# Staging weights in other buffers and spreading their splitting into the first block: a fused Mamba and mixture-of-experts layer on one Trainium2 core

## The reference

```python
xn = _layernorm(x)
# branch 1: Mamba (E = 512 channels, N = 16 states, 4 convolution taps)
hidden, gate = split(einsum('blh,he->bel', xn, W_in))
hidden = silu(causal_conv(hidden) + conv_bias)
dt, Bm, Cm = split(einsum('ble,ed->bld', hidden^T, W_x))
dts = softplus(dt @ W_dt + b_dt)
state = exp(dts * A) * state + dts * Bm * hidden      # over time, for 16 states
y = (sum over states of state * Cm + hidden * D) * silu(gate)
out1 = y @ W_out
# branch 2: top-8 of 32 experts, evaluated densely with zero weights for the rest
probs = softmax(xn @ router_w.T);  rw, sel = top_k(probs, 8);  rw = rw / sum(rw)
for e in experts: acc += silu(xn @ w_gate[e]) * (xn @ w_up[e]) @ w_down[e] * w_e
return x + out1 + acc
```

## Time and profile before

| | us |
|---|---|
| median of 3 runs | 1395.14 (1394.36 to 1397.05) |
| profiled execution, its own time | 1396.65 |
| its span | 1394.8 |
| outside the span | 1.85 |
| PE busy | 1319.1 (95%) |
| POOL busy | 1243.4 (89%) |
| DVE busy | 1233.4 (88%) |
| ACT busy | 1215.1 (87%) |

### The profile page before, as it was taken

How to read it: one execution, slowest core, us unless ns; L and a number is a source line. 1 busy time by engine, 2 the same in 40 slices (tenths; PEclk the granted TensorE clock), 3 DMA queues, 4 the chain that set the end, 5 groups by cost and what they waited for, 6 DMA issues and landing times.

```text
span 1394.8 us, 26557 instructions
## 1 busy us (share of the span) xinstructions
PE 1319.1 (95%) x9314; PEld 1237.2 (89%) x9314; DVE 1233.4 (88%) x1580; ACT 1215.1 (87%) x2054; POOL 1243.4 (89%) x641
## 2 busy tenths in 40 slices
PE   2499999999999999999999999999999999999998
PEld 2389998999989999999989999898999989999987
DVE  4498989999899999989899898999989899898886
ACT  3799988989998898888989998888989989998884
POOL 3689998999989998999998989898998989999996
PEclk9899999999999999999999999999999999999999
DMA  6634444434444444344434444433343443434342
GB/s 158 171 96 129 119 124 130 118 116 122 124 115 125 124 115 131 112 136 119 127 113 126 128 113 125 130 113 120 114 135 110 129 120 118 134 108 131 118 133 68
DMA packets 184531, 170.74 MB, mean 122 GB/s; under 512 B 42672, under 2 KB 167632, under 8 KB 184400
## 3 DMA queue, kind: packets, MB, share of 16 engines
q1 hardware_dynamic: 150608, 121.86, 30.0%
q10 hardware_dynamic: 33792, 47.20, 12.5%
HBM read 163.72 MB, written 5.24 MB: 121 GB/s over the span
## 4 chain that ended last, share of the span: by engine, by line
PE 30%; ACT 25%; DVE 20%; issue 13%; POOL 10%; ACTq 1%; DMA 1%; SPq 0%; DVEq 0%; POOLq 0%
PE pair_ps L851 12%; ACT decay L553 8%; PE out_ps L969 7%; DVE state L752 7%; ACT L553 6%; POOL state L467 4%; DVE u L769 3%; DVE moe L776 3%; DVE acc L759 3%; PE front_ps L851 3%; PE turn_ps L931 3%; PE front_ps L894 2%; ACT L561 2%; ACT moe L561 2%; POOL moe L482 2%
## 5 line engine op out<-in xcount | busy, mean ns | idle before, releaser
L752 DVE TENSOR_TENSOR_SCAN state<-decay,state 128x512 f32<-128x512 f32 x512 | 616.0, 1214 | 95.0 <-ACT decay L553 88.5
L467 POOL TENSOR_TENSOR state<-du,b_rep 128x1024 f32<-128x1024 f32 x256 | 608.0, 2384 | 72.0 <-DVE u L769 71.8
L553 ACT ACTIVATE decay<-dt,neg_a 128x255 f32<-128x255 f32 x1024 | 437.0, 467 | 61.6 <-DVE state L752 47.1
L969 PE MATMUL out_ps<-w_down,moe 128*128 128x256 f32 x1536 | 353.2, 379 | 2.0 <-POOL moe L482 2.0
L969 PEld LDWEIGHTS out_ps<-w_down,moe 128*128 128x128 f32 x1536 | 284.4, 190 | 38.4 <-issue 3.6
L482 POOL TENSOR_TENSOR moe<-moe,rw_rep 128x512 f32<-128x512 f32 x192 | 260.3, 1367 | 22.6 <-DVE moe L776 22.2
L476 POOL TENSOR_TENSOR state<-state,c_rep 128x1024 f32<-128x1024 f32 x96 | 251.7, 2622 | 11.0 <-DVE state L752 10.9
L851 PE MATMUL pair_ps<-xnT_hi,w_up_hi 128*128 128x256 f32 x768 | 232.8, 303 | 15.9 <-ACT moe L561 13.5
L851 PE MATMUL pair_ps<-xnT_hi,w_gate_hi 128*128 128x256 f32 x768 | 229.5, 299 | 7.1 <-DVE moe L776 7.1
L553 ACT ACT_TABLE_LOAD x176 | 225.8, 1283 | 3.2
L851 PE MATMUL pair_ps<-xnT_hi,w_up_lo 128*128 128x256 f32 x768 | 217.6, 283 | 0.0
(11 more groups left out here) (97 smaller groups left out, 2095.2 us busy)
## 6 DMA issues: line engine op xcount, KB each, us to landing
w_down<-in_L_ffn_w_down_dram SPq DMA_DIRECT2D x384, 128.0 KB, 2.5
b_rep<-b_dram ACTq DMA_DIRECT2D x128, 256.0 KB, 3.5
rw_rep<-rw_dram SPq DMA_DIRECT2D x256, 96.0 KB, 2.7
rw_rep<-rw_dram SPq DMA_DIRECT2D x256, 64.0 KB, 2.7
c_rep<-b_dram ACTq DMA_DIRECT2D x96, 128.0 KB, 3.0
rw_rep<-rw_dram SPq DMA_DIRECT2D x256, 32.0 KB, 2.5
x_in<-L_attn_input_states_dram SPq DMA_DIRECT2D x16, 256.0 KB, 3.3
res<-L_attn_input_states_dram SPq DMA_DIRECT2D x16, 256.0 KB, 3.6
```

Of the source, the lines that this page charges most:

```text
L467: pool.tensor_tensor(state[:, n % STATES, :, :], du2[:, q, :, :], b_rep[:, n // BCH % 2, n % BCH, :][:, None, :].broadcast_to([P, ET, T]), ...
L553: last = act.activation(decay[:, h, j, 1:T], dt[:, q, e, 1:T], ACT.Exp, scale=neg_a[:, e, n:n + 1])
L752: dve.tensor_tensor_scan(x, decay[:, h, :, :].rearrange("p e t -> p (e t)"), x, 0.0, ALU.mult, ALU.add).then_inc(scanned, 1)
L969: last = pe.matmul(out_ps[:, c, :], moe[:, p % RING, j, c * P:(c + 1) * P], w_down[:, p % RING, j, :], start=(p == 0 and j == 0 and c == 0 ...
```

## The change

Three things are changed together.

1. `staging` is six buffers instead of four: the halves of `u2`, `dt` and `du2` that the odd blocks use, `gate2`, and two halves of `w_down`. Piece k goes to buffer k mod 6. None of these is used by block 0 before its middle.
2. The waits follow the buffers. POOL's first `state_input` no longer waits for the splits. In its place SP waits for all splits ahead of the first loads of `w_down`, ACT ahead of `hid0` of block 1 and ahead of the first gate. On SP the load of x for block 1 moves to just before piece 9's, and that of `w_out` to just behind piece 17's. Splits may stand in block 0's own slots.
3. All slot tables hold new numbers, for the splits and for the work of every block.

```diff
-    UNIT_AT = [0, 2, 8, 24, 30, 33, 42, 44, 47, 55, 55, 56, 56, 61, 70, 84, 87, 102, 102, 107, 107, 112, 119, 119]
+    UNIT_AT = [-5, 1, 6, 18, 18, 28, 37, 41, 41, 53, 54, 57, 61, 61, 64, 85, 86, 87, 112, 113, 114, 115, 119, 121]
...
-    SPLIT_VECTOR_AT = [-109, -101, -93, -90, -69, -46, -44, -37, -36]
-    SPLIT_SCALAR_AT = [-126, -113, -108, -106, -106, -96, -95, -68, -65, -60, -53, -46, -39, -39, -36, -26, -23, -20]
-    SPLIT_POOL_AT = [-107, -101, -101, -92, -69, -69, -32, -29, -18]
+    SPLIT_VECTOR_AT = [-124, -96, -91, -56, -51, -35, -35, -5, 14]
+    SPLIT_SCALAR_AT = [-124, -119, -103, -99, -81, -78, -77, -77, -58, -39, -37, -37, -30, -22, -3, -1, 4, 11]
+    SPLIT_POOL_AT = [-102, -96, -86, -84, -64, -57, -37, -6, 7]
...
-        staging = [state[:, m, :, :].rearrange("p e t -> p (e t)") for m in range(STATES)]
+        staging = [x[:, 1, :, :].rearrange("p e t -> p (e t)") for x in (u2, dt, du2)]
+        staging.append(gate2[:, :, :].rearrange("p e t -> p (e t)"))
+        STAGED_DOWN = UT * P // WGROUPS
+        staging += [w_down[:, :, :, :].rearrange("p r j h -> p (r j h)")[:, m * STAGED_DOWN:(m + 1) * STAGED_DOWN] for m in range(2)]
...
+                if k == 9:
+                    sp.wait_ge(front_filled, 1)
+                    load_x(1)
+            sp.dma_start(w_out[:, :, :], w_out_d.rearrange("(k p) h -> p k h", p=P)).then_inc(w_late_loaded, 16)
             sp.wait_ge(rw_stored, 16)
             for p in range(WEIGHTS - 1):
                 load_rw(0, p)
+            wait_split(sp, len(splits))
             for p in range(RING):
                 load_down(p)
-            sp.wait_ge(front_filled, 1)
-            load_x(1)
-            sp.dma_start(w_out[:, :, :], w_out_d.rearrange("(k p) h -> p k h", p=P)).then_inc(w_late_loaded, 16)
...
                 if n == 0:
                     pool.wait_ge(du_ready, i + 1)
-                    if first_pair(i):
-                        wait_split(pool, len(splits))
...
+                    if name == "hid0" and i == 1:
+                        wait_split(act, len(splits))
...
+                if half == 0 and first_pair(i):
+                    wait_split(act, len(splits))
...
+            def split_scalar(k):
+                act.wait_ge(staged[k % len(staging)], (k // len(staging) + 1) * 16)
+                act.activation(splits[k][0], staged_part(k), ACT.Copy).then_inc(split_hi, 1)
```

More of the change, by code:

```diff
@@ L79, in build @@
-    GATE_AT = [44, 56]
-    SILU_AT = [-2, 13, 24, 36, 44, 48, 63, 75, 92, 95, 112, 115]
-    SCALAR_FRONT = {'xnT': -115, 'hid0': -107, 'hid1': -99, 'weightsT': -64, 'low': -53, 'lowT': -50, 'dt0': -44, 'dt1': -32}
-    CONV_SILU_AT, ROUTER_EXP_AT, SOFTPLUS_AT, FIRST_AT, SKIP_AT = [-66, -86, -23, 4, 19]
-    GATE_SILU_AT = [46, 62]
-    MUL_AT = [14, 29, 45, 49, 56, 63, 77, 89, 106, 110, 124, 129]
-    ADD_AT = [[23, 27], [36, 37], [52, 59], [72, 74], [81, 93], [101, 109], [113, 116], [123, 126], [130, 132]]
@@ L102, in build @@
-    SPLIT_POOL_AT = [-107, -101, -101, -92, -69, -69, -32, -29, -18]
+    UNIT_AT = [-5, 1, 6, 18, 18, 28, 37, 41, 41, 53, 54, 57, 61, 61, 64, 85, 86, 87, 112, 113, 114, 115, 119, 121]
+    OUT_AT = [38, 38, 46, 61, 74, 98, 99, 101, 117, 124, 141, 145]
+    TURN_AT = [[8, 10], [18, 18], [31, 33], [51, 52], [65, 69], [80, 81], [106, 109], [114, 116], [118, 119], [126, 126]]
+    TURN_Y_AT, PROJECT_AT = [130, 130], 159
+    PE_FRONT = {'xnT': -111, 'hid0': -108, 'hid1': -94, 'logits': -89, 'weightsT': -62, 'low': -51, 'lowT': -47, 'dt0': -38, 'dt1': -23}
@@ new lines, in build @@
+    GATE_AT = [56, 62]
+    SILU_AT = [-1, 12, 25, 39, 42, 51, 63, 72, 92, 95, 112, 113]
+    SCALAR_FRONT = {'xnT': -114, 'hid0': -107, 'hid1': -99, 'weightsT': -62, 'low': -56, 'lowT': -50, 'dt0': -37, 'dt1': -25}
+    CONV_SILU_AT, ROUTER_EXP_AT, SOFTPLUS_AT, FIRST_AT, SKIP_AT = [-67, -73, -21, 7, 17]
+    GATE_SILU_AT = [61, 63]
+    MUL_AT = [15, 21, 41, 46, 54, 62, 69, 82, 110, 111, 122, 128]
+    ADD_AT = [[21, 22], [36, 50], [53, 64], [71, 77], [99, 102], [106, 111], [114, 118], [123, 126], [129, 129]]
@@ L512, in slot @@
                     tap_sum(i, q)
+                for k, at in zip(range(1, len(splits), 2), SPLIT_POOL_AT):
+                    if i == 0 and a == at:
+                        split_lo(pool, k)
             for a in range(-SLOTS, 0):
                 slot(0, 0, a)
-                for k, at in zip(range(1, len(splits), 2), SPLIT_POOL_AT):
-                    if a == at:
-                        split_lo(pool, k)
             blocks(pool, slot)
@@ L661, in slot @@
                     skip(i, q)
+                for k, at in enumerate(SPLIT_SCALAR_AT):
+                    if i == 0 and a == at:
+                        split_scalar(k)
             for a in range(-SLOTS, 0):
                 slot(0, 0, a)
-                for k, at in enumerate(SPLIT_SCALAR_AT):
-                    if a == at:
-                        act.wait_ge(staged[k % len(staging)], (k // len(staging) + 1) * 16)
-                        act.activation(splits[k][0], staged_part(k), ACT.Copy).then_inc(split_hi, 1)
             blocks(act, slot)
@@ L829, in slot @@
                     total(i)
+                for k, at in zip(range(0, len(splits), 2), SPLIT_VECTOR_AT):
+                    if i == 0 and a == at:
+                        split_lo(dve, k)
             for a in range(-SLOTS, 0):
                 slot(0, 0, a)
-                for k, at in zip(range(0, len(splits), 2), SPLIT_VECTOR_AT):
-                    if a == at:
-                        split_lo(dve, k)
             blocks(dve, slot)
```

16 lines of the change are left out of this document (6 added, 10 removed).

## The result

| | before | changed |
|---|---|---|
| median, same chip, 4 runs each | 1396.1 (1394.36 to 1397.79) | 1433.79 (1432.89 to 1435.6) |
| span of the profiled execution | 1394.8 | 1431.7 |

The ratio is 1.0272, with a 95% interval from 1.0254 to 1.0289: slower by 37.7 us. Forecast was 1383.5, faster by 11.6, in a range that ended at 1397.

A forecast was written before the change was run, and what follows sets the result against it. PE was taken to bound the repeating blocks, a latency chain the start. From the profiled 1396.65 us, -6.0 for the start and -5.6 for 14 blocks gave 1385.05; the median, 1.5 lower, 1383.5, range 1373 to 1397.

The forecast's parts named there:

- What bounds the kernel: Repeating blocks: PE bounds them, busy 81.8 of 83.0 us, so reordering can give back at most 1.2 us a block.
- the walk of the repeating part: One block of the new order, followed with old durations: closes at 82.1 us, no better than 1 us.
- the term of -5.6 for 14 blocks: Repeating part: -0.4 us a block, taken from the walk's -0.9, makes -5.6 us in all.
- PE waits where one block meets the next: Rival, block boundary: turn_y and first turn wait for DVE, slower overall from +0.43 us a block, 1409 at +1.4; chance 0.18.
- The start: Front and block 0 up to the first scan of state 3: -6.0 us, after which block 0 is PE's.
- The tail: Last block: it keeps its tail, so 0 us.
- The head: Head of the front: an earlier first DVE split lets hid0 start at 14.0, not 16.2 us: -2.2.
- The softplus: Front, on ACT: no wait for a transfer, softplus ends at 49.6 against 55.4 us: -5.8 in all.
- The first scan: Start of scanning on DVE in block 0: at 55.2 us instead of 62.95, -7.8.
- the first scan of state 3: Block 0, on DVE: at about 69.5 us against 75.46 before, -6.0 left after the late splits' cost.
- SP's and ACT's new waits: Block 0 and later: they cost nothing while SP's margin of about 2 us holds, otherwise up to 2 us on POOL's queue.
- Slower: Whole kernel above 1397.9 us, from +0.63 us a block on: chance 0.14, all from the block-boundary rival.

The follow-up runs named there:

- e7: Changed kernel with POOL's state x C products and expert weightings made on half their columns (timing only); 1377.19 us, ratio 0.9855.
- e8: Kernel before the change with POOL's state x C products and expert weightings made on half their columns (timing only); 1380.38 us, ratio 0.9877.
- e10: Changed kernel with 12 unread matmuls added on PE ahead of its wait for weightsT in each block; 1415.35 us, ratio 1.0123.
- e14: Changed kernel with 12 unread matmuls ahead of PE's wait for weightsT and the last routing product on ACT; 1397.60 us, ratio 1.0005.
- e6: Changed kernel with the last routing product made by ACT, as two scaled copies, instead of DVE; 1396.51 us, ratio 0.9999.
- e5: Changed kernel with the routing on DVE seven slots earlier (-67, not -60); 1414.90 us, ratio 1.0133.
- e3: Kernel before the change with the change's tables for the blocks, its own staging, waits and split tables; 1439.65 us, ratio 1.0311.
- e9: Changed kernel with the old tables for the blocks, keeping the change's staging, waits, early first pieces and late splits; 1392.12 us, ratio 0.9958.
- e1: Changed kernel with every slot table as before, splits included, keeping six buffers, waits and load order; 1393.05 us, ratio 0.9979.

## Why the prediction was wrong

**What bounds the kernel** was right for the kernel before: in e7 and e8 a block is 81.7 to 81.8 us, near PE's own busy time in the earlier trace rows (81.77 of 83). It did not follow that the new order would be bound by the same engine.

**The step that failed** is the walk of the repeating part, in its first two sentences: "The instructions are the same ... so only waits can change. I walked one block of the new order by hand with the durations of the rows." Durations changed: DVE's by 3.9 us a block, at the same instructions. The means of add_row and of the routing product, 1.6 and 1.8 us, were no property of the instruction, but of who stood beside it in the old order. Both had a wide range in the trace of before: 1.19 to 2.32 us for the product, 1.20 to 3.35 for add_row. The walk came to 82.1 us, the repeating block is 85.39; the term of -5.6 for 14 blocks was +33.0. Two parts make it up by the runs, and leave almost nothing over: 1.25 us a block for the clock that falls behind PE's new wait (e10), 1.10 for the routing's last product on DVE (e14 against e10). Longer durations alone are not the loss: e6 and e14 keep the long add_row and repeat in 83.0 us, as before. Nor is the place alone: e5 moves the routing forward and repeats in 84.08. By these runs the loss needs both, a fuller DVE and tables that put its routing behind PE's place for it.

The walk had the right rule before it. The prediction cited the Trainium skill's page "SBUF — State Buffer" (Who interferes with whom) for the splits: two SBUF inputs on DVE and an SBUF read on POOL exclude each other. The routing's product, ending with POOL's instruction, agrees. (`x_in` has one tensor input; the page names such instructions in their two-port modes too. Its 0.41 us free of POOL and 2.43 beside it would fit; which mode it ran in, no run here shows.) It named neither add_row nor the routing products, which are of that kind, and gave the rule no case of its own in the repeating part. By the earlier trace rows POOL was busy 76.56 of 83 us, so that most such instructions meet one.

**The waits named were not the ones that came.** "PE waits where one block meets the next" had the sign and the right kind, but another place and more than the price it was given (2.36 a block against at most 1.4): `turn_y`'s wait is gone, the wait is at `weightsT`, which the walk did not follow. That the clock falls after it stood in no case.

**The start.** Here too the sum failed: -6.0 was forecast, with block 0 given as PE's from state 3 on, and at the second table load the changed kernel is 2.3 us behind (-4.4 and +6.7). e3, with all splits done early, already has 81.8 us for that interval, against 77.6 before, so 4.2 of the 6.7 come with the new tables; how the other 2.5 divide among late splits and `x_in` no run shows. The tail, taken as 0, was +1.6.

The head was given -2.2 and came to -0.23 (`hid0` at 16.00, before 16.23). Piece 1 was there in time; the 2 us went to `x_in`, 2.68 us beside POOL's split. The forecast's 14.0 is what e9 shows, 14.03. The softplus was to end at 49.6, 5.8 us earlier. No transfer stands in its chain any more, as forecast, and it is 4.4 us earlier (du starts at 51.00, before at 55.41); the 1.4 that are missing are less than the 2.0 lost in the head. The first scan at 56.50 was forecast for 55.2, before was 62.95. At the first scan of state 3, forecast 69.5, it is 75.63, as before (75.46): block 0 has taken all back in that trace, though not mainly through splits (1.88 and 1.82 us on DVE), but through `x_in` again, 4.23 us. The mechanism of the start is sound with the old tables: e9 is 5.8 us ahead at the second table load, and 4.6 in the medians. That the change is 5.9 us faster than e3 is near the forecast's -6.0 in part by luck, since e3 starts 4.6 us later than the kernel before. No cost of SP's and ACT's new waits is seen: e1 and e9 have them, and both are faster than before.

**The chances.** Slower had 0.14, and all of it hung on one mechanism. For an order in which four engines are near 90% busy, each change of neighbours can be dearer than all gains together; the bound of +1.4 us a block came from the waits alone and let no duration move.
